# Moving x1's deviation and bias sum ahead of the input subtractions on GpSimd, in a two-pass attention and MLP kernel

## The reference

```python
def _inorm(x):
    return (x - mean(x)) * rsqrt(var(x) + EPS)          # along each row
# layer 0, per item
Mn = Wn @ _inorm(x_c) + bn;  Mm = Wm @ _inorm(x_s) + bm
A  = softmax(Mn.T @ Mm)
x1 = Wo @ ((Wl @ x_s + bl) @ A.T) + bo + x_c
# layer 1, per item
q = layer_norm(x1, ln1_w, ln1_b) @ q_w + q_b            # k, v from ctx
out = softmax(q @ k.T / sqrt(32)) @ v                   # 16 heads
hidden = out @ cproj_w + cproj_b + x1
y = gelu(layer_norm(hidden, ln2_w, ln2_b) @ fc_w + fc_b) @ proj_w + proj_b
return hidden + y
```

## Time and profile before

| what | value |
|---|---|
| runs | 3034.43 us median (3033.48 to 3048.21) |
| the profiled execution | 3045.41 us, span 3043.6 us |
| TensorE matmul (PE) busy | 2862.2 us, 94% |
| VectorE (DVE) busy | 1880.3 us, 62% |
| ScalarE (ACT) busy | 1495.3 us, 49% |
| GpSimd (POOL) busy | 1121.4 us, 37% |
| DMA packets | 416.66 MB, mean 137 GB/s |
| granted TensorE clock, mean | 0.982 |

### The profile page before, as it was taken

The page is one execution under the profiler, slowest core; times in us unless marked ns, Lnnn a source line. Parts: engine busy times, 40 slices in busy tenths (PEclk is TensorE's granted clock), DMA queues, the critical chain, the costliest instruction groups (busy, mean ns, idle before and its releaser), DMA issues. The chain is left out here.

```text
span 3043.6 us, 54525 instructions
## 1 busy us (share of the span) xinstructions
PE 2862.2 (94%) x17527; PEld 2370.5 (78%) x17527; DVE 1880.3 (62%) x3642; ACT 1495.3 (49%) x4274; POOL 1121.4 (37%) x998
## 2 busy tenths in 40 slices
PE   5899999999999999999976999999999999999999
PEld 4777777777777777777765888888888888888887
DVE  5788888888888888888865433333333333333332
ACT  5788877888788887888753211111111111111111
POOL 4566666666666666666642000000000000000000
PEclk7899999999999999999997999999999999999999
DMA  6588888888888888888764211101111111111110
GB/s 188 161 231 224 230 223 240 229 236 229 234 235 234 232 225 236 235 232 232 213 188 141 70 28 28 38 31 41 41 41 41 28 28 37 32 41 41 41 28 14
DMA packets 440891, 416.66 MB, mean 137 GB/s; under 512 B 155201, under 2 KB 319553, under 8 KB 440769
## 3 DMA queue, kind: packets, MB, share of 16 engines
q1 hardware_dynamic: 440768, 415.40, 49.6%
HBM read 231.79 MB, written 167.77 MB: 131 GB/s over the span
## 5 line engine op out<-in xcount | busy, mean ns | idle before, releaser
L1346 ACT ACTIVATE gl<-pre,fc_bias 128x512 f32<-128x512 f32 x256 | 176.6, 690 | 1118.9 <-PE pre L1431 1118.9
L1385 DVE CAST hT_hi<-gl 128x512 fp32r<-128x512 f32 x256 | 109.1, 426 | 838.6 <-ACT gl L1346 838.6
L685 ACT ACTIVATE rows<-bank,negmax 128x128 f32<-128x128 f32 x1024 | 365.1, 395 | 126.7 <-DVE negmax L865 126.7
L607 POOL TENSOR_TENSOR at_lo<-a_blocks,at_hi 128x512 fp32r<-128x512 f32 x256 | 338.7, 1345 | 192.5 <-ACT at_hi L730 192.5
L593 POOL TENSOR_TENSOR rows<-rows,rsum 128x512 f32<-128x512 f32 x256 | 266.6, 1042 | 272.9 <-DVE rsum L861 272.8
L177 POOL TENSOR_TENSOR rstd<-ve,neghalf 128x4 f32<-128x4 f32 x16 | 16.3, 1019 | 869.0 <-DVE ve L171 869.0
L1429 PE MATMUL pre<-yT_lo,rest_hi 128*128 128x512 f32 x768 | 298.8, 389 | 0.0
L1430 PE MATMUL pre<-yT_hi,rest_lo 128*128 128x512 f32 x768 | 298.8, 389 | 0.0
L1431 PE MATMUL pre<-yT_hi,rest_hi 128*128 128x512 f32 x768 | 298.8, 389 | 0.0
L1429 PE MATMUL acc<-rest_lo,hT_hi 128*128 128x512 f32 x768 | 298.8, 389 | 0.0
L1430 PE MATMUL acc<-rest_hi,hT_lo 128*128 128x512 f32 x768 | 298.8, 389 | 0.0
(11 more groups left out here) (159 smaller groups left out, 7891.8 us busy)
## 6 DMA issues: line engine op xcount, KB each, us to landing
a_turn<-rows SPq DMA_DIRECT2D x128, 512.0 KB, 7.6
a_blocks<-a_turn SPq DMA_DIRECT2D x256, 256.0 KB, 5.1
p_turn<-rows SPq DMA_DIRECT2D x128, 512.0 KB, 5.0
p_blocks<-p_turn SPq DMA_DIRECT2D x256, 256.0 KB, 5.8
x_ctx<-in_x SPq DMA_DIRECT2D x64, 256.0 KB, 2.7
x_ctx<-in_ctx SPq DMA_DIRECT2D x64, 256.0 KB, 2.9
blocks<-in_ctx SPq DMA_DIRECT2D x256, 64.0 KB, 5.6
small<-in_x SPq DMA_DIRECT2D x64, 256.0 KB, 6.0
```

What stands on the lines that cost most here:

```text
L607: pool.tensor_tensor(by_rows(at_lo, j), a_chunks[:, j], by_rows(at_hi, j).bitcast(F32), ALU.subtract).then_inc(at_lo_set, 1)
L685: act.activation(probs[:, :, r, c, :], by_chunk(S1_BANK[r])[:, c, :].rearrange("p (d b) -> p d b", b=32), ACT.Exp, bias=negmax1[:, r, c:c ...
L1346: act.activation(gl[:, i % 2, :], pre[i % 2][:], ACT.Gelu_apprx_tanh, bias=mlp.fc_bias[:, i:i + 1]).then_inc(gelu_done, 1)
```

## The change

GpSimd's inverse deviation of x1 and its sum with the projection's bias are issued before the two subtractions of `lower_normed` instead of behind them, in all slots that are not filling. Nothing else is altered.

```diff
                 lower_at(0)
                 lower_at(1)
-                if not filling:
-                    lower_normed()
                 if b1.exists():
                     pool.wait_ge(x1_veps, b1.nth(1, 1))
...
                     pool.tensor_tensor(x1b[:, b1.quarter, :], x1[:], cproj_bias[:], ALU.add).then_inc(x1b_set, 1)
+                if not filling:
+                    lower_normed()
                 if a1.exists():
                     pool.wait_ge(ctxT_hi_set, a1.nth(1, 1))
```

## The result

The changed kernel takes 3089.02 us, median of four runs (3081.66 to 3103.08); the kernel before took 3039.26 beside it (3033.48 to 3048.21). The ratio is 1.0162 [1.0138, 1.0185]: slower by 1.6%, where 0.9% of the median was forecast. The profiled execution took 3081.66 us (span 3079.8), 36.3 us more than the 3045.41 of before; 16.5 were forecast.

A forecast was written before the change was run, and what follows sets the result against it. Two nearly equal rings, compute 23.7 and DMA 23.4 us, were taken to bound the kernel; 55 slots x (24.2 - 23.9) = +16.5 us on 3045.4 gave 3062 us, range 3012 to 3092.

The forecast's parts named there:

- Compute ring 22.7: Loop through ScalarE, TensorE, VectorE and GpSimd: x1's turn starts earlier, 0.95 us off each slot, leaving 22.7 us.
- L911 held by the first normed_lo only: VectorE's normalisation of x1 meets only GpSimd's first normed_lo, ending near 811.8 instead of 813.1 through the second.
- rival 3: x1's normalisation is held through both normed_lo, its turn hardly moves: 3034 to 3045 us, chance 0.13.
- D + 22.4: From a block on, GpSimd's next at_lo starts 22.4 us after the end of VectorE's inputs' normalisation (D).
- 22.4 + 1.6 = 24.0: Slot with one of VectorE's two input normalisations held by at_lo: at_lo's start plus 1.6 us, 24.0 us.
- 22.4 + 3.0 = 25.4: Slot with both of VectorE's input normalisations held by at_lo: at_lo's start plus 3.0 us, 25.4 us.
- Blocks, and their shares 35/35/30: Slots with none, one or two input normalisations held by GpSimd: 35, 35 and 30%, mean 24.2 us.
- Now it waits for 808.22 ... ends 0.6 us later; I take 0: GpSimd's new wait for x1's variance delays its later work 0.6 us; cost through the a_blocks read 0, at most 0.7.
- No block 23.4: Slot with no held normalisation, by early landing or TensorE's lower clock level behind a long wait: 23.4 us.
- Rival 2: The DMA ring sets the slot at 23.4 us without held normalisations: 16 us gained, 3018 us, chance 0.15.
- the DMA ring: Loop from inputs' normalisation through SyncE's loads, a_turn write and a_blocks reads back to VectorE: 23.4 us, not shortened.
- rival 1: Full gain: the DMA ring shortens too, by 0.7 us; 52 us off the median, 2982 us, chance 0.10.

The follow-up runs named there:

- e7: Changed kernel with a_turn's writes ahead of the next loads on SyncE's queue and the third at_lo ahead of x1's deviation: 2977.59 us, ratio 0.9792.
- e10: Changed kernel with a_turn's writes first, the third at_lo early, and GpSimd's first at_lo waiting for the inputs' normalisation: 2976.32 us, ratio 0.9794.
- e1: Changed kernel with GpSimd waiting for the inputs' normalisation before its first at_lo: 3032.2 us, ratio 0.9966.

## Why the prediction was right in its course and short in its size

- **Compute ring 22.7**: right. Where nothing else bound (e7, e10) the slots last 22.67 and 22.66.
- **L911 held by the first normed_lo only**: right, as the slot at 801.82 shows and 52 of the 53 counted L911, which end 0.28 or 0.29 us behind it (one was not held); rival 3 fell.
- **"D + 22.4", the start of at_lo in a blocked slot: this step failed.** It is the term that was sized too short. 22.43 is the lowest of the 37 values; the mean is D + 22.69 (22.67 before one block, 22.71 before two). I had counted 22.4 from a block, and the slot before is not always blocked. Ten slots began with at_lo 0.33 to 0.56 behind D, those that follow the ten unblocked slots at TensorE's lower clock. There the next at_lo came one turn of the compute ring later, after 22.5 to 22.8 us, at D + 23.03 to 23.14, and six of them were blocked: 4 us of what is missing. The other 31 values lie between 22.43 and 22.66 but for three. (20 x 0.27 + 17 x 0.31) / 53 = 0.20 us a slot, 55 x 0.20 = 11 us of the missing 20.
- **"22.4 + 1.6 = 24.0" and "22.4 + 3.0 = 25.4"**: the holds, from at_lo's start to D, measured 1.71 (1.57 to 1.86) and 2.99 us. So 3.0 was right and 1.6 short by 0.11, because the first at_lo takes up to 1.58 us instead of 1.28 when it begins while VectorE's first normalisation runs. That makes another 2 us.
- **Blocks, and their shares 35/35/30**: nearly right, measured 30/38/32. With these shares and the lengths of the forecast the mean would be (16 x 23.4 + 20 x 24.0 + 17 x 25.4) / 53 = 24.27 instead of 24.21, 3 us. The last 3 come from the kernel before, whose counted slots are 23.84 where I used 23.9.
- **"Now it waits for 808.22 ... ends 0.6 us later; I take 0"**: a little too low. Behind a_turn's landing the read went out 0.11 us later than before (0.19 against 0.08). The blocked slots, whose length is at_lo's start and the hold, do not contain it; in e1, where the ring bounds every slot, it is 0.15 of the 0.2 us over 23.4.
- **No block 23.4**: 23.35, right, and by both of its reasons: in six of the 16 VectorE waited for a_blocks, ten stand behind two blocks and TensorE's lower clock. Rival 2, the DMA ring without blocks (16 us gained), is what e1 does, with 8.5 us gained, mostly because of the second path; rival 1, the full gain (2982), needed two more edits (2977.59).
- TensorE's wait for the mask grew by (75.6 - 33.7) / 54 = 0.8 us a slot, where I expected about 1.

The shape of the hold was the point at which trace and rule were weighed. The rows: every L911 and L895 between 183 and 1480 us in the two profiles that takes 0.60 us or more (61 before, 105 after) ends 0.28 to 0.29 us after a GpSimd instruction's end. The Trainium skill (SBUF — State Buffer, section "SBUF: two separate sides") states such a hold: the port pair that VectorE and GpSimd share is "an exclusive lock, not a bandwidth split", held for a whole instruction by a GpSimd instruction or by a VectorE one in a two-port mode or with two SBUF inputs, whichever starts first. The trace agrees as to the hold, though L895 ends 0.28 us behind the GpSimd instruction, less than the 0.53 that it takes alone; in which mode L895 runs, no run here shows. The page says it more sharply than the one that the prediction weighed against the rows; the hold's length in the sum came from the earlier trace rows in any case, and would have been the same.

What stays open: why at_lo follows D by 22.45 or by 22.6 in otherwise equal slots was not tried, and why the granted clock fell behind 11 of the slots with two blocks and not behind the other six is not shown.

## What to carry to other kernels

Taking a wait off one ring of a software pipeline moves every engine on that ring earlier against those that are not on it: before such a move, list the pairs of VectorE and GpSimd instructions whose order rested on slack alone, and give the slower ring its time first. A transfer that waits for two things gains only when both come earlier; look at the queue's own waits for the second. And where a term is the start of something in a ring that jumps between states, take its mean over the states in which the turn before can end, not its value behind one of them.

## What the runs showed of the hardware

The hold is by single instructions and is passed on at each end: of two GpSimd instructions back to back, a held VectorE instruction of 0.53 us gets in between (L895 twice behind at_lo twice: 2.95 us for the pair, not 0.98 after both). In all 166 cases of the two profiles it ends 0.28 to 0.29 us behind the GpSimd instruction's end, and GpSimd's next is late by 0.15 (2.71 for two at_lo instead of 2.56). The other way round, an at_lo that begins while L895 runs takes up to 1.58 us instead of 1.28, and that L895 keeps its 0.53. VectorE's transposes show no such stretch beside the same work: the pair of L902 at 1016.07, behind the block, takes 1.29 with at_lo still to run out beside it, and 1.30 at 1035.95 without; none of the 212 in the changed kernel takes over 0.72. And behind two blocks a stretch at the granted clock of 0.50, like that from 825.2 to 828.6, moved the next at_lo from D + 22.5 or 22.6 to D + 23.74 to 24.01.
